# An adaLN block with a state-space layer and a channel mix: the first three batches and the last one scheduled anew

## The reference, cut to what matters

```python
mod = (silu(c) @ wmod).reshape(16, 6, 1, 256)       # sa, ca, ga, sb, cb, gb
h = layernorm(x) * (1 + ca) + sa
u, gate = split(h @ W_in.T)
b_t = u @ W_state.T
dt = minimum(softplus(u @ W_dt.T + b_dt), 10)
decay = exp(-dt * (softplus(A_log) + 1e-4))
s[t] = decay[t] * s[t-1] + (1 - decay[t]) * b_t[t]   # 512 steps
z = (s @ W_C.T) * silu(gate) + h * D
x = x + clamp(ga) * (z @ W_out.T)
h = layernorm(x) * (1 + cb) + sb                     # second norm
xk, xr = mu_k * h + (1 - mu_k) * h_prev, the same with mu_r
k = square(relu(xk @ W_k.T))
x = x + clamp(gb) * sigmoid(xr @ W_r.T) * (k @ W_v.T)
```

## Time and profile before

| what | value |
|---|---|
| median of 3 runs | 375.15 us (374.97 to 375.49) |
| the profiled execution | 375.2 us |
| its span in the trace | 373.4 us |
| TensorE matmul busy | 359.3 us (96%) |
| VectorE, ScalarE, GpSimd busy | 303.2, 307.7, 259.3 us (81, 82, 69%) |
| granted TensorE clock | 1.00 |

### The profile page before, as it was taken

The page is one execution under the profiler, slowest core; times in us unless marked ns, Lnnn a source line. Parts: engine busy times, 40 slices in busy tenths (PEclk is TensorE's granted clock), DMA queues, the critical chain, the costliest instruction groups (busy, mean ns, idle before and its releaser), DMA issues.

```text
span 373.4 us, 5613 instructions
## 1 busy us (share of the span) xinstructions
PE 359.3 (96%) x1702; PEld 275.8 (74%) x1705; DVE 303.2 (81%) x640; ACT 307.7 (82%) x416; POOL 259.3 (69%) x269
## 2 busy tenths in 40 slices
PE   7999799999999999999999999999999999999784
PEld 4776477777778777777778777777877777776563
DVE  2788967988979798988979898888979788877654
ACT  4466779899898989989898989989898989977372
POOL 2072658969686887969686986968687894855560
PEclk9999999999999999999999999999999999999999
DMA  8931111130313132040313122040303021010111
GB/s 280 395 109 56 56 59 56 58 114 0 117 53 112 59 108 61 32 139 2 113 57 114 56 73 97 2 141 29 114 0 114 1 76 38 21 38 0 56 55 60
DMA packets 18607, 29.16 MB, mean 78 GB/s; under 512 B 1168, under 2 KB 9616, under 8 KB 18448
## 3 DMA queue, kind: packets, MB, share of 16 engines
q1 hardware_dynamic: 18144, 28.71, 22.6%
q10 hardware_dynamic: 432, 0.09, 0.1%
HBM read 20.40 MB, written 8.39 MB: 77 GB/s over the span
## 4 chain that ended last, share of the span: by engine, by line
POOL 46%; issue 39%; PE 7%; DVE 4%; ACT 2%; DMA 1%; POOLq 1%; SPq 0%; DVEq 0%; ACTq 0%
POOL xr_lo L773 10%; POOL xk_lo L773 7%; POOL z_lo L830 6%; POOL h_lo L773 6%; POOL k_lo L773 6%; POOL state_lo L820 4%; POOL rstd L783 3%; PE slot L224 3%; DMA w_in<-weights_in 1%; PE slot L238 1%; PE slot L352 1%; DVE stats L566 1%; POOL prev L814 1%; POOL spread L781 1%; POOL spread L780 1%
## 5 line engine op out<-in xcount | busy, mean ns | idle before, releaser
L809 POOL TENSOR_TENSOR rstd<-mv,half_neg 128x4 f32<-128x4 f32 x16 | 16.1, 1007 | 54.0 <-DVE mv L579 54.0
L452 ACT ACTIVATE prev<-slot,mod,mix_prev 128x512 f32<-128x512 f32 x64 | 46.3, 787 | 5.8 <-PE slot L231 5.8
L773 POOL TENSOR_TENSOR xk_lo<-xk,xk_hi 128x512 fp32r<-128x512 f32 x32 | 40.9, 1298 | 9.8 <-ACT xk_hi L463 9.0
L224 PE MATMUL slot<-h_hi,wf_hi 128*128 128x512 f32 x128 | 45.9, 399 | 0.4 <-ACT h_hi L478 0.4
L224 PE MATMUL slot<-h_hi,wf_lo 128*128 128x512 f32 x128 | 45.6, 397 | 0.0
L773 POOL TENSOR_TENSOR xr_lo<-xr,xr_hi 128x512 fp32r<-128x512 f32 x32 | 42.5, 1330 | 0.0
L830 POOL TENSOR_TENSOR z_lo<-z,z_hi 128x512 fp32r<-128x512 f32 x26 | 33.7, 1295 | 10.9 <-ACT z_hi L459 7.4
L773 POOL TENSOR_TENSOR k_lo<-k_act,k_hi 128x512 fp32r<-128x512 f32 x30 | 38.2, 1293 | 3.8 <-ACT k_act L533 3.8
L773 POOL TENSOR_TENSOR h_lo<-h,h_hi 128x512 fp32r<-128x512 f32 x30 | 38.4, 1303 | 3.1 <-ACT h_hi L478 3.1
L231 PE MATMUL slot<-ident,xn 128*128 128x128 f32 x256 | 35.9, 274 | 2.8 <-DVE xn L603 2.1
L231 PEld LDWEIGHTS slot<-ident,xn 128*128 128x128 f32 x256 | 29.7, 141 | 11.3 <-issue 4.7
(11 more groups left out here) (123 smaller groups left out, 1002.5 us busy)
## 6 DMA issues: line engine op xcount, KB each, us to landing
x_tok<-x_tok_in SPq DMA_DIRECT2D x16, 512.0 KB, 3.6
x_ch<-x_ch_in SPq DMA_DIRECT2D x16, 512.0 KB, 3.7
x_out<-wmod SPq DMA_DIRECT2D x15, 512.0 KB, 3.0
wmod<-wmod_in SPq DMA_DIRECT2D x1, 1024.0 KB, 10.1
w_in<-weights_in SPq DMA_DIRECT2D x1, 1024.0 KB, 11.5
w_in<-weights_in SPq DMA_DIRECT2D x1, 768.0 KB, 5.6
wmod<-wmod_in SPq DMA_DIRECT2D x1, 512.0 KB, 6.6
x_out<-wmod SPq DMA_DIRECT2D x2, 256.0 KB, 2.0
```

The source lines that it names most:

```text
L224: ins = nc.tensor.matmul(out, w[:, c, at + d * P:at + (d + 1) * P], x[:, c, :], start=first, stop=last)
L452: return nc.scalar.activation(prev[:, mix, i, 1:T + 1], ps_n[:, i, :], ACT.Identity, bias=mod_at(SHIFT2 + i, k), scale=mix_prev[:, mix, i, ...
L773: nc.gpsimd.tensor_tensor(lo, x, hi.bitcast(F32), ALU.subtract).then_inc(done, 1)
L809: nc.gpsimd.tensor_tensor(rstd2[:, c % 2], mv2[:, c % 2, 1, :], half_neg[:], ALU.pow).then_inc(rstd2_ok, 1)
```

## The change

The loop starts at step 3, and what steps 0 to 2 did is written out one by one on each engine. The front and gate of batch 0 are whole (float32), so batch 0 needs no `h_hi` and `h_lo`. The front and gate of batch 2 are done ahead of the loop. PSUM slots of the first three batches rotate otherwise, and in the loop gate, second norm and K are in slot 2 and x1 and V in slot 3. The early weights are loaded in two parts (512 and 256 KB), and the rest of wmod goes before tokens 2. Zero matmuls: 14 in place of 32. In the loop `xr_lo[0]` goes ahead of `state_hi`. In the last batch: x1 is transposed before the `xk_lo` part of batch 14, ScalarE applies half of the second norm, K is whole and by output halves, `prev` is made KEY first, relu and squares go by halves, `k_lo[0]` is GpSimd's, and each output half of V is finished before the other begins.

```diff
-        ps_h, ps_front, ps_y = slot[0], slot[0], slot[0]
+        ps_front, ps_y = slot[0], slot[0]
...
+        def ps_h(k):
+            return slot[1] if 0 < k <= WHOLE else slot[0]
...
-            sp.dma_start(w_in[:, 0:CH * 3 * C], w_d[:, 0:CH * 3 * C]).then_inc(s_w, 16)
+            sp.dma_start(w_early[:, :, 0:GATE], w_early_d[:, :, 0:GATE]).then_inc(s_w, 16)
...
+            sp.dma_start(w_early[:, :, GATE:], w_early_d[:, :, GATE:]).then_inc(s_wgate, 16)
...
@@ TensorE, beginning
-            keep_warm(slot[0][:, 0, :], 13)
+            keep_warm(slot[0][:, 0, :], 10)
...
+            first_norm(0)
+            keep_warm(slot[3][:, 0, :], 4)
+            half(dt_out, w_front, 0, h[:, 0], 0, first=True)
+            half(dt_out, w_front, 0, h[:, 0], 1, last=True).then_inc(dt_ps, 1)
+            half(b_out, w_front, NS, h[:, 0], 0, first=True)
+            half(b_out, w_front, NS, h[:, 0], 1, last=True).then_inc(b_ps, 1)
...
+            half(g_out, w_early, GATE, h[:, 0], 0, first=True)
+            half(g_out, w_early, GATE, h[:, 0], 1, last=True).then_inc(g_ps, 1)
+            modulation(4, 3, slot[2][:, 1, :])
+            state_out(0)
+            first_norm(1)
+            modulation(7, 5, slot[2][:, 1, 3 * NB:]).then_inc(mod_ps, 1)
+            attention_out(0, 0)
+            front_high(1)
+            front_low(1)
+            attention_out(0, 1)
+            gate_high(1)
+            gate_low(1)
+            first_norm(2)
+            token_stats(0)
+            state_out(1)
+            gate_high(2)
+            front_high(2)
+            to_channels(ps_n, xn2).then_inc(t3_ps, 1)
+            front_low(2)
+            gate_low(2)
+            attention_out(1, 0)
+            attention_out(1, 1)
@@ TensorE, loop
+                if d == LAST:
+                    for j in range(CH):
+                        for i in range(CH):
+                            pe.wait_ge(xk_ok[i], d + 1)
+                            last = half([k_out[j]], w_late, MIX_K + j * P, xk, i, first=(i == 0), last=(i == CH - 1))
+                        last.then_inc(k_half_ps if j == 0 else k_ps, 1)
...
+                if c == LAST:
+                    token_stats(c)
...
+                if live(d):
+                    pe.wait_ge(xrlo_ok[0], d + 1)
+                    half(r_out, wl_hi, MIX_R, xr_lo, 0)
                 if live(b):
                     if split(b):
                         pe.wait_ge(shi_ok, b - WHOLE + 1)
...
-                if live(d):
-                    pe.wait_ge(xrlo_ok[0], d + 1)
-                    half(r_out, wl_hi, MIX_R, xr_lo, 0)
                 if split(b):
                     pe.wait_ge(slo_ok, b - WHOLE + 1)
...
+                    for j in range(CH):
+                        for i in range(CH):
+                            pe.wait_ge(khi_half_ok[i], 1)
+                            half([v_out(d)[j]], wl_hi, MIX_V + j * P, k_hi, i, first=(i == 0))
+                            half([v_out(d)[j]], wl_lo, MIX_V + j * P, k_hi, i)
+                        for i in range(CH):
+                            pe.wait_ge(klo_ok[i], d + 1)
+                            last = half([v_out(d)[j]], wl_hi, MIX_V + j * P, k_lo, i, last=(i == CH - 1))
+                        last.then_inc(v_half_ps if j == 0 else v_ps, 1)
@@ ScalarE, end
+                if c == LAST:
+                    act.wait_ge(shift2_ok, 1)
+                    for t in range(TT // 2, TT):
+                        last = nc.scalar.activation(xn2[:, t, :], ps_x1(c)[:, t, :], ACT.Identity, bias=shift2[:, t:t + 1], scale=rstd2[:, c % 2, t:t + 1])
+                    last.then_inc(xn2b_ok, 1)
...
+                    previous(KEY, 0, c).then_inc(prev_ok[0], 1)
...
+                    previous(KEY, 1, c).then_inc(prev_ok[1], 1)
@@ VectorE, beginning (behind the weight split and the rate)
-            dve.wait_ge(hhi_ok, 1)
+            ln1_stats(1)
+            clipped(0)
+            ln1_mean_variance(1)
+            driven(0)
+            scanned(0)
+            ln1_apply(1)
+            ln1_stats(2)
+            ln1_mean_variance(2)
+            gated(0)
+            ln1_apply(2)
             for i in range(CH):
-                nc.vector.tensor_tensor(h_lo[:, i], h[:, 0, i], h_hi[:, i].bitcast(F32), ALU.subtract)
+                dve.wait_ge(hhi_ok, 1)
+                nc.vector.tensor_tensor(h_lo[:, i], h[:, 1, i], h_hi[:, i].bitcast(F32), ALU.subtract)
+            rest_of_modulation()
+            clipped(1)
+            ln1_stats(3)
+            after_attention(0)
+            driven(1)
+            scanned(1)
+            ln1_mean_variance(3)
+            after_transpose(0)
+            gated(1)
+            normalised(0)
+            ln1_stats(4)
+            ln1_mean_variance(4)
+            ln1_apply(3)
+            mixing(0, 0)
+            clipped(2)
+            mixing(0, 1)
+            after_attention(1)
+            driven(2)
+            scanned(2)
+            after_transpose(1)
```

More of the change, by code:

```diff
@@ new lines, in state_out, with attention_out @@
+            def state_out(k):
+                pe.wait_ge(state_ok, k + 1)
+                for i in range(CH):
+                    last = nc.tensor.matmul(ps_y[:, i, :], w_y[:, i * P:(i + 1) * P], state[:], start=True, stop=True)
+                last.then_inc(y_ps, 1)
+            def attention_out(k, i):
+                pe.wait_ge(h_ok, k + 2)
+                pe.wait_ge(z_ok[i], k + 1)
+                last = half(o_out, w_late, OUT, z, i, first=(i == 0), last=(i == CH - 1))
+                if i == CH - 1:
+                    last.then_inc(o_ps, 1)
@@ L409, in _ @@
+                if live(a):
+                    first_norm(a)
+                if live(d) and d < LAST - 1:
+                    pe.wait_ge(klo_ok[0], d + 1)
+                    half(v_out(d), wl_hi, MIX_V, k_lo, 0)
                 if live(b):
-                    if b == 0:
-                        pe.wait_ge(s_wl, 16)
                     before(pe, tanh_ok, d + 1 if live(d) else 0)
@@ L421, in _ @@
                         half(o_out, w_late, OUT, z, 0, first=True)
-                if live(d) and d < LAST:
+                if live(d) and d < LAST - 1:
                     pe.wait_ge(klo_ok[1], d + 1)
-                    half(v_out, wl_hi, MIX_V, k_lo, 1, last=True).then_inc(v_ps, 1)
+                    half(v_out(d), wl_hi, MIX_V, k_lo, 1, last=True).then_inc(v_ps, 1)
                 if split(b):
@@ L449, in gate, with ln1_apply @@
                 nc.scalar.activation(r_gate[:], ps_r[:], ACT.Tanh, scale=0.5).then_inc(tanh_ok, 1)
+            def ln1_apply(k):
+                act.wait_ge(shift1_ok, k + 1)
+                before(act, t1_ps, k)
+                for t in range(TT // 2):
+                    last = nc.scalar.activation(xn1[:, t, :], x_tok[:, k % 3, t, :], ACT.Identity,
+                                                bias=shift1[:, k % 2, t:t + 1], scale=rstd1[:, k % 2, t:t + 1])
+                last.then_inc(xn1a_ok, 1)
             def previous(mix, i, k):
@@ new lines, in mixing, with mixing_last @@
+            def mixing(k, i):
+                if i == 0:
+                    dve.wait_ge(first_ok, k + 1)
+                dve.wait_ge(prev_ok[i], k + 1)
+                for x, mix, done, low in ((xk, KEY, xk_ok, xklo_ok), (xr, REC, xr_ok, xrlo_ok))[::1 if i == 0 else -1]:
+                    before(dve, low[i], k)
+                    mixed(x, mix, i, k, done[i])
+            def mixing_last(k):
+                dve.wait_ge(first_ok, k + 1)
+                for n, (x, mix, done, low) in enumerate(((xk, KEY, xk_ok, xklo_ok), (xr, REC, xr_ok, xrlo_ok))):
+                    for i in range(CH):
+                        dve.wait_ge(prev_ok[i], k + 1 + n)
+                        dve.wait_ge(low[i], k)
+                        mixed(x, mix, i, k, done[i])
@@ new lines, in low_state, with low_h @@
+            def low_state(k):
+                pool.wait_ge(shi_ok, k - WHOLE + 1)
+                pool.wait_ge(y_ps, k)
+                nc.gpsimd.tensor_tensor(state_lo[:], state[:], state_hi[:].bitcast(F32), ALU.subtract).then_inc(slo_ok, 1)
+            def low_h(k):
+                for i in range(CH):
+                    pool.wait_ge(hhi_ok, k)
+                    pool.wait_ge(g_ps, k)
+                    nc.gpsimd.tensor_tensor(h_lo[:, i], h[:, k % 2, i], h_hi[:, i].bitcast(F32), ALU.subtract).then_inc(hlo_ok[i], 1)
@@ L812, in _ @@
-                    for x_done in (*xk_ok, *xr_ok):
-                        before(pool, x_done, c)
-                    nc.gpsimd.tensor_copy(prev[:, :, :, 0], mix_first[:, :, :, c]).then_inc(first_ok, 1)
-                if live(d):
+                    second_scale(c)
+                if live(d) and c != LAST:
                     low_part(xr_lo[:, 1], xr[:, 1], xr_hi[:, 1], xrhi_ok[1], r_ps, xrlo_ok[1], d)
-                if split(b):
-                    pool.wait_ge(shi_ok, b - WHOLE + 1)
-                    pool.wait_ge(y_ps, b)
```

(10 more changed lines are left out.)

579 lines of the change are left out of this document (354 added, 225 removed).

## The result

The changed kernel takes **369.57 us** (369.45 to 369.72, 4 runs) beside 375.32 us for the kernel before (374.97 to 376.06, 4 runs): ratio 0.984 [0.983, 0.986], 5.75 us faster. The forecast was 368.8.

The account below looks back on a forecast made before the run. TensorE's own list bounds the middle, so time could come only from the two ends: 2.9 + 0 + 3.5 = 6.4 us off a 373.4 span, 367.0, with 1.8 around it 368.8 us; range 366.0 to 372.3 (0.8).

Parts of the forecast that it names:

- The beginning: Start of the kernel up to step 4 of the loop: 2.9 us gained, bounds 1 and 4.5.
- Items 1 to 4: Beginning, from first weights through batch 0's exponential and scan to h of batch 1: at 23.1, 4.4 us earlier.
- item 1: First weights, 512 KB in place of 768, land 0.65 us earlier: fold at 6.2, modulation 8.0, h of batch 0 11.1.
- item 5: Beginning, behind h of batch 1: part given back through waits and added products, K of batch 0 at 49.2, 1.4 later.
- Item 6: Step 3 without batch 2's front and gate (5.6 us): second-norm transposes at 58.1, 3.3 earlier; 2.9 ahead at step 4.
- The whole product: An unsplit float32 product on TensorE costs 0.86 us by the row, three fp32r 0.70; the four-pass rule would give 0.93.
- The middle: 13 loop steps with `xr_lo[0]` ahead of `state_hi`: value 0, at best a gain of 0.1 us a step (1.3).
- Rival A: Slower: `state_lo` loses its cover on TensorE in all 13 loop steps, 7.2 us, giving 376.0; chance 0.07.
- Rival B: The beginning gives nothing, as VectorE's list and step 3's waits take it back; only the end remains, 371.7; chance 0.16.
- The end: Batch 15 and what follows K of batch 14: last VectorE chain starts 3.5 us earlier, bounds 2 and 4.5.
- Rival D: The end gives only 1.5 us, as ScalarE's six half operations become its bound: 370.8; chance 0.10.
- Rival C: TensorE's clock falls to half level between 16 and 46 us, with 18 fewer zero matmuls: up to 389; chance 0.02.

Follow-up runs that it names:

- experiment 10: The kernel before with only the early weights' load split in two (512 KB, then the gate's 256 KB): 375.70 us, ratio 1.001.
- experiment 7: The changed kernel with K of batch 15 split again into high and low parts, output halves kept: 371.72 us, ratio 0.990.
- experiment 2: The changed kernel with only the loop's order undone, `xr_lo[0]` between `state_hi` and `state_lo` again: 369.38 us, ratio 0.985.
- experiment 5: The changed kernel with `k_lo` of batch 14 between the two halves of K of batch 15: 368.86 us; repeated 368.97 us.
- experiment 9: The changed kernel with GpSimd's scale of batch 1's second norm ahead of its `state_lo` of batch 2: 369.91 us, ratio 0.986.
- experiment 1: The changed kernel with its end alone undone (all of batch 15 as in the kernel before): 373.26 us, ratio 0.995.
- experiment 4: The changed kernel with 1 zero matmul in place of 10 ahead of the fold: 374.39 us, ratio 0.994.
- (6): The changed kernel with the second norm of batch 15 applied by VectorE alone: 370.07 us, ratio 0.986.

## Why the prediction was right, and where it was short

Step by step, in us from the span's start; the two columns on the right are the two profiles of the changed kernel:

| step | predicted | first | repeat |
|---|---|---|---|
| fold | 6.2 | 6.11 | 6.16 |
| modulation | 8.0 | 8.48 | 8.06 |
| h of batch 0 | 11.1 | 11.36 | 11.04 |
| exponential | 13.9 | 14.27 | 13.96 |
| scan | 17.2 | 17.60 | 17.28 |
| state product | 20.1 | 20.48 | 20.16 |
| h of batch 1 | 23.1 | 23.36 | 23.04 |
| K of batch 0 | 49.2 | 49.75 | 49.41 |
| transposes, second norm | 58.1 | 58.95 | 58.62 |
| K of batch 1 | 65.5 | 66.24 | 65.90 |
| step of the middle | 21.2 | 21.21 | 21.21 |
| last VectorE chain | 361.6 | 362.29 | 361.97 |

The forecast was 6.4 us, and the first profile has 2.15 + 0.28 + 3.31 = 5.7. The 0.28 of the middle was not forecast: by luck it covers part of what the two ends lack (5.5 of 6.4).

**The beginning**: 2.9 forecast, 2.15 and 2.49 measured. Items 1 to 4 hold to a tenth in the repeat, whose fold ran at full pace; VectorE's statistics of batch 1, now ahead of the clip, start at 13.18 and in the repeat at 12.86 (13.0 forecast). The first profile is 0.4 later from the modulation on: the term that failed there is item 1's unspoken one, that the fold takes the 1.83 us of the earlier trace rows in every execution. It depends on when TensorE comes to full pace, and the prediction treated the zeros as free filler. In item 5 the gate of batch 2 waits 0.31 for its `h_hi` (0.9 forecast) and the front 0.78 for z of batch 1 (0.6); K of batch 0 is 1.6 to 1.95 later in place of 1.4. Item 6 was mis-sized by 0.3: K to the transposes takes 9.2, not 8.9.

That the first weights land earlier is seen (fold at 6.11 and 6.16, was 6.86), and the 0.65 taken between 0 and 0.91 was near. That it shortens the kernel was not shown by itself (experiment 10). And item 1 left out the next load, `wmod`. Where the first weights land earlier still, the modulation waits for it instead. This is the profile of experiment 7, whose beginning has the same instructions:

```profile
5.83 1.99 PE L348 MATMUL slot<-w_in 128*128 128x256 f32 x8 [0.17 <-DMA w_in<-weights_in]
8.40 1.96 PE L258 MATMUL slot<-c_silu,wmod 128*128 128x16 f32 x16 [0.58 <-DMA wmod<-wmod_in]
```

The fold is 0.33 earlier than in the repeat and the modulation 0.34 later. The same wait is 0.22 us in experiment 2, 0.31 in the repeat of experiment 5 and 0.62 in experiment 9.

**The whole product** at 0.86 held at three places: twice in the beginning, and in the end, where four and the four fp32r of `k_lo` take 357.07 - 352.63 = 4.44 (4 x 0.86 + 4 x 0.233 = 4.37). The Trainium skill (FP8 and Floating Point Precision, TensorE Precision Notes) counts 4 passes for true FP32. With 0.233 for a pass, as the prediction took it, an estimate of the same stretch is 4.66; the trace does not agree. But it does not speak against the count either: the bf16 zeros at full pace are 0.22 apart, and four times that is 0.87. The prediction's rival price took fp32r's distance for that of a pass. And the reason given for the edit's worth held: what it costs TensorE (8 x 0.16 in the beginning) is less than the waits it removes. Split again, the beginning lost 1.2 us and the end about 2.

**The middle**: 0 forecast, 0.28 measured, and experiment 2 shows that the reordering is not its source. Its first step is 0.13 shorter (K of batch 2 comes 21.11 behind K of batch 1, was 21.24); the rest is spread over the others, and the cause stays open. `state_lo` starts 0.27 behind the last matmul with `state_hi`, hardly more than the dense 0.233, so its cover held as worked out:

```profile
121.86 0.40 PE L489 MATMUL slot<-state_hi,wy_lo 128*128 128x512 f32 x1
122.13 0.73 PE L495 MATMUL slot<-state_lo,wy_hi 128*128 128x512 f32 x2
```

**Rival A** fell by its own criterion: steps of 21.21, not over 21.5. **Rival B** fell with K of batch 1 at 66.24 and with experiment 1, in which the beginning alone gives 2.1 us.

**The end**: 3.5 forecast, 3.31 measured. Counted from K of batch 14, the prediction's marks and the trace's: transposes of x1 2.3 and 2.26, norm applied 8.1 and 8.06, K of batch 15 10.7 and 10.67, relu 15.3 and 15.45, last chain 20.1 and 20.33. Of the missing 0.2, 0.14 is there at the relu, since the whole K and `k_lo` of batch 14 take 4.44 in place of 4.3; the rest lies behind it: V's first half starts right behind R, at 359.88, and has to wait for VectorE's `k_lo` (0.28 us). **Rival D** (ScalarE's six half operations as the bound) is not what is seen: the last chain starts 362.29 - 355.74 = 6.55 us behind K, under the 7 of its mark. These end at 360.86, as forecast, but the item that set them off, `k_lo` of batch 14 ahead of the relu, was a cost that the prediction accepted and experiment 5 took away. The parts of the end by themselves: whole product about 1.7 to 2.2 us (7), shared norm 0.5 to 0.6 (6), both measured within the rest of the new end; the remainder of the 3.3 (transposes of x1 first, KEY first, V by halves) was not tried part by part.

**Rival C** (the clock) had a place and price that were not met: in both profiles of the changed kernel the pace stayed full between 16 and 46 us. But the half level costs time in this kernel at two other places: in the end of experiment 1, 0.7 us behind a gap of 2.1 us, and ahead of the fold, where experiment 4 lost 4.8 us by the medians. The one execution at 370.89, some 1.3 us above the others, has a mean clock of 0.995 and no profile, so where it lost that time is not known.

Two of the prediction's sums do not come out of its own lines. Rival A's 0.15 for the exposed load is 0.34 - 0.233 = 0.11 by the rows, which makes its time 375.3 and not 376.0. And half of A with the small losses is 0.065 for no change, half of A with C is 0.055 for slower, where it says 0.05 and 0.07. Neither touches the forecast.

## What to carry to other kernels

Where a float32 product has few consumers and stands on a chain through several engines, the unsplit product can win although it is longer on TensorE: price it by the start-to-start distance in the trace, and price the split one with its rounding, its subtraction and their waits. When a chain is shortened, ask at once which list decides next; here it was TensorE's own in the beginning, and in the end a product of another batch queued ahead of what ScalarE waited for, worth 0.6 to 0.7 us by moving four matmuls. Work done only to keep TensorE busy before the first weights is not filler: time its removal over many runs, since it shows in some and not in others.
